# Score products of a graph layer per batch, with high and low parts side by side in one stationary block

## What is computed

```python
z_l = h @ W_lang.T;  z_g = h @ W_grav.T;  v = h @ W_V.T
zn  = z_l / max(norm(z_l), EPS)
A_l = max(zn @ zn.T, 0) * not_eye                        # 64 x 64 for each batch
d2  = max(sq + sq.T - 2 * z_g @ z_g.T, 0)                # sq = row sums of z_g * z_g
A_g = exp(-d2 / (2 * sigma**2)) * not_eye
K   = w * rows(A_l * causal) + (1 - w) * rows(A_g * causal)   # rows divided by their sums
out = (K @ v) @ W_O.T
x   = layernorm(x + out)
```

## Time and profile before

| | |
|---|---|
| median of 3 runs | 684.94 us (684.61 to 684.97) |
| profiled execution, its own time | 685.29 us |
| its span | 683.5 us, mean granted clock 0.996 |

### The profile page before, as it was taken

The page is one execution under the profiler, slowest core; times in us unless marked ns, Lnnn a source line. Parts: engine busy times, 40 slices in busy tenths (PEclk is TensorE's granted clock), DMA queues, the critical chain, the costliest instruction groups (busy, mean ns, idle before and its releaser), DMA issues.

```text
span 683.5 us, 11745 instructions
## 1 busy us (share of the span) xinstructions
PE 669.0 (98%) x3579; PEld 571.0 (84%) x3579; DVE 532.2 (78%) x1523; ACT 345.6 (51%) x614; POOL 210.4 (31%) x454
## 2 busy tenths in 40 slices
PE   7999999999999999999999999999999999999994
PEld 6888888888888888888888888888888888888883
DVE  5935697878879787887968787796978779697786
ACT  4734445464454546455454645545474554545433
POOL 0222315051341515134151513416051331503022
PEclk9999999999999999999999999999999999999998
DMA  7201102011110201111020111102011110001002
GB/s 280 107 7 57 61 32 94 1 62 63 56 68 31 92 0 61 61 61 61 31 92 0 64 59 61 61 31 92 0 66 57 61 61 31 32 0 63 1 31 94
DMA packets 20406, 38.33 MB, mean 56 GB/s; under 512 B 1824, under 2 KB 1824, under 8 KB 20384
## 3 DMA queue, kind: packets, MB, share of 16 engines
q1 hardware_dynamic: 20384, 38.05, 15.3%
HBM read 21.27 MB, written 16.78 MB: 56 GB/s over the span
## 4 chain that ended last, share of the span: by engine, by line
PE 92%; DVE 3%; ACT 2%; DMA 1%; issue 1%; POOL 1%; SPq 0%; POOLq 0%; DVEq 0%
PE ring L357 56%; PE bank_p L377 12%; PE ring L475 4%; PE bank_x L318 3%; PE bank_p L318 3%; PE bank_k L421 3%; PE bank_r L421 3%; PE bank_pt L390 2%; PE bank_r L397 1%; DMA w_raw<-in_L_gnn_W_lang_dram 1%; PE bank_pt L336 1%; PE bank_r L336 1%; PE bank_k L336 1%; PE bank_pt L408 1%; PE bank_x L336 1%
## 5 line engine op out<-in xcount | busy, mean ns | idle before, releaser
L562 ACT ACTIVATE yT_hi<-ring 128x512 fp32r<-128x512 f32 x128 | 75.9, 593 | 113.5 <-PE ring L357 113.3
L357 PE MATMUL ring<-hT_hi,T_hi 128*128 128x512 f32 x320 | 130.5, 408 | 0.6 <-DVE hT_lo L772 0.5
L357 PE MATMUL ring<-hT_hi,T_lo 128*128 128x512 f32 x320 | 125.4, 392 | 0.0
L357 PE MATMUL ring<-hT_lo,T_hi 128*128 128x512 f32 x320 | 124.7, 390 | 0.0
L777 DVE TENSOR_TENSOR yT_lo<-ring,yT_hi 128x512 fp32r<-128x512 f32 x128 | 87.5, 684 | 35.3 <-ACT yT_hi L562 35.3
L357 PE MATMUL ring<-M_hi,hT_hi 128*128 128x512 f32 x256 | 101.5, 396 | 0.0
L357 PE MATMUL ring<-M_hi,hT_lo 128*128 128x512 f32 x256 | 100.2, 391 | 0.0
L357 PE MATMUL ring<-M_lo,hT_hi 128*128 128x512 f32 x256 | 99.9, 390 | 0.0
L1084 POOL TENSOR_SCALAR z_ve<-z_mv 128x2 f32<-128x2 f32 x32 | 7.0, 218 | 268.8 <-DVE z_mv L873 264.1
L1077 POOL TENSOR_TENSOR x_lo<-x_sb,x_hi 128x512 fp32r<-128x512 f32 x60 | 76.4, 1301 | 22.4 <-ACT x_hi L562 22.4
L614 ACT ACTIVATE o_sb<-o_sb,z_nb,z_rs 128x512 f32<-128x512 f32 x60 | 47.2, 810 | 62.3 <-POOL z_nb L1089 62.3
(11 more groups left out here) (159 smaller groups left out, 1390.6 us busy)
## 6 DMA issues: line engine op xcount, KB each, us to landing
x_sb<-in_x_dram SPq DMA_DIRECT2D x15, 1024.0 KB, 5.2
out_dram<-o_sb SPq DMA_DIRECT2D x60, 256.0 KB, 2.0
x_sb<-in_x_dram SPq DMA_DIRECT2D x2, 512.0 KB, 5.5
w_raw<-in_L_gnn_W_lang_dram SPq DMA_DIRECT2D x1, 1024.0 KB, 6.7
o_sb<-in_L_gnn_W_grav_dram SPq DMA_DIRECT2D x1, 1024.0 KB, 9.4
h_sb<-in_L_gnn_W_V_dram SPq DMA_DIRECT2D x1, 1024.0 KB, 11.6
w_raw<-in_L_gnn_W_O_dram SPq DMA_DIRECT2D x1, 1024.0 KB, 7.9
out_dram<-x_sb SPq DMA_DIRECT2D x4, 256.0 KB, 2.0
```

The source lines that it names most:

```text
L357: last = pe.matmul(bank[:, :], a, b, start=n == 0, stop=n == len(terms) - 1)
L562: return act.activation(dst, src, ACT.Copy, scale=scale)
```

## The change

`gram` before had one 128 x 128 stationary block for each of high and low `hT` and did 3 x 4 matmuls of 256 columns a pair (24 for a call). After, `hT` holds for each pair the four blocks [high of batch 0, low of batch 0, low of batch 1, high of batch 1], 64 columns each, so that a stationary block of 128 columns is the high and the low part of one batch; the moving operand is [y high, y low] x [L, G] x 64 columns of the same batch. That is 2 x 4 matmuls of 256 columns a pair, 16 for a call, and only the diagonal blocks are computed. The result has the four quarters high·high, high·low, low·high and low·low in different partitions and columns. ACT copies the high rows (`Q_sb`, two copies of 64 x 512), POOL adds high·high and high·low (`Q_sum`), and DVE adds low·high from PSUM and writes P (`merge`, two instructions of 64 x 256). ACT also copies the high parts of `hT` into a contiguous `hU`, which is the stationary block of the u projections. The result of a call takes two PSUM banks, so the banks of `transpose_h` move, and the second `gram` of a step waits for the `merge` of the first.

```diff
+        hT = [sb(f"hT{i}", [R, DC, NP, 4, N], fp32r) for i in range(2)]
+        hT_hi = [t[:, :, :, 0:4:3, :] for t in hT]
+        hT_lo = [t[:, :, :, 1:3, :] for t in hT]
+        hU = sb("hU", [R, DC, GT], fp32r)
+        yT = sb("yT", [R, DC, 2, 2, GT], fp32r)
...
+                elif p == 3:
+                    pe.wait_ge(hT_split, NP * g + 1)
...
                 elif q:
-                    pe.wait_ge(p_copied, 2 * g + q)
+                    pe.wait_ge(p_merged, 2 * g + q)
...
                 for pp in range(2):
-                    s = slice((2 * q + pp) * R, (2 * q + pp + 1) * R)
-                    terms = [(a[:, i, s], b[:, i, :, s]) for i in range(DC)
-                             for a, b in parts(hT_hi[par], hT_lo[par], yT_hi, yT_lo)]
-                    for n, (a, b) in enumerate(terms):
-                        last = pe.matmul(p_bank(g, q)[:, pp, :, :], a, b, start=n == 0, stop=n == len(terms) - 1)
+                    p = 2 * q + pp
+                    for b in range(2):
+                        t = slice((2 * p + b) * N, (2 * p + b + 1) * N)
+                        for i in range(DC):
+                            last = pe.matmul(q_banks(g, q)[:, pp, b, :, :, :], hT[par][:, i, p, 2 * b:2 * b + 2, :],
+                                             yT[:, i, :, :, t], start=i == 0, stop=i == DC - 1)
...
+            def copy_hU(g, par, p):
+                act.wait_ge(hT_hi_done, NP * g + p + 1)
+                copy(hU[:, :, p * R:(p + 1) * R].rearrange("p c (b t) -> p c b t", b=2),
+                     hT_hi[par][:, :, p, :, :]).then_inc(hU_ready, 1)
...
+            def copy_q(g, q):
...
+                    act.wait_ge(q_summed, 2 * g + q)
+                for b in range(2):
+                    rows = slice(b * N, (b + 1) * N)
+                    last = copy(Q_sb[rows, :, :, :, :], q_banks(g, q)[rows, :, b, :, :, :])
+                last.then_inc(q_copied, 1)
...
                 hi_proj(g, 5)
+                copy_hU(g, par, 0)
+                copy_hU(g, par, 1)
                 hi_proj(g, 6)
+                copy_hU(g, par, 2)
+                copy_hU(g, par, 3)
                 hi_proj(g, 7)
...
+            def merge(g, q):
+                dve.wait_ge(q_summed, 2 * g + q + 1)
...
+                for b in range(2):
+                    rows, other = slice(b * N, (b + 1) * N), slice((1 - b) * N, (2 - b) * N)
+                    last = dve.tensor_tensor(P_sb[q][rows, :, :, rows], q_banks(g, q)[other, :, b, 0, :, :],
+                                             Q_sum[rows, :, :, :], ALU.add)
+                last.then_inc(p_merged, 1)
...
+            def sum_q(g, q):
+                d = 2 * g + q
+                pool.wait_ge(q_copied, d + 1)
...
+                pool.tensor_tensor(Q_sum[:, :, :, :], Q_sb[:, :, 0, :, :], Q_sb[:, :, 1, :, :],
+                                   ALU.add).then_inc(q_summed, 1)
...
+                    sum_q(g - 1, 1)
                     columns(g - 1, 1)
...
+                sum_q(g, 0)
                 columns(g, 0)
```

More of the change, by code:

```diff
@@ L98, in bass_two_layer_graph_resnorm @@
         h_sb = [sb(f"h_sb{i}", [R, NP, D]) for i in range(2)]
[L100 to L104, removed]
+        hT = [sb(f"hT{i}", [R, DC, NP, 4, N], fp32r) for i in range(2)]
[3 more added lines that the diff above has]
+        yT = sb("yT", [R, DC, 2, 2, GT], fp32r)
         u_hi = sb("u_hi", [R, NP, D], fp32r)
         u_lo = sb("u_lo", [R, NP, D], fp32r)
+        Q_sb = sb("Q_sb", [R, 2, 2, 2, N])
+        Q_sum = sb("Q_sum", [R, 2, 2, N])
         P_sb = [sb(f"P_sb{q}", [R, 2, 2, R]) for q in range(2)]
@@ L241, in bass_two_layer_graph_resnorm, with is_last, q_banks, hT_bank @@
         block = ctx.enter_context(nc.Block())
-        def p_bank(g, q):
-            return last_p_ps if isinstance(g, int) and g == NG - 1 and q else p_ps
+        def is_last(g):
+            return isinstance(g, int) and g == NG - 1
+        def q_banks(g, q):
+            return last_q_ps if is_last(g) and q else q_ps
+        def hT_bank(g, p):
+            if isinstance(g, int) and g == 0:
+                return (bank_x, bank_k, bank_pt, bank_r)[p]
+            return (bank_pt, bank_k, bank_r, bank_pt)[p]
+        def row_bank(g):
+            return last_row_ps if is_last(g) else row_ps
         def out_rows(g):
@@ L313, in layer0 @@
                     pe.wait_ge(y_added, NP * g + p - 1)
-                elif p == 1 and not (isinstance(g, int) and g < 2):
-                    pe.wait_ge(p_copied, 2 * g - 2)
+                elif p == 0 and not (isinstance(g, int) and g < 2):
+                    pe.wait_ge(p_merged, 2 * g - 2)
                 bank = (bank_x, bank_p)[p % 2]
@@ L362, in gram @@
                 pe.wait_ge(proj_split, NPROJ * g + 2 * DC)
-                if isinstance(g, int) and g == NG - 1:
-                    if not q:
-                        pe.wait_ge(p_copied, 2 * g)
+                if is_last(g):
+                    if q:
+                        pe.wait_ge(z_added, NP * g)
+                    else:
+                        pe.wait_ge(p_merged, 2 * g)
                 elif q:
-                    pe.wait_ge(p_copied, 2 * g + q)
+                    pe.wait_ge(p_merged, 2 * g + q)
                 else:
@@ L556, in proj_dst @@
                 return (u_hi, u_lo)[which][:, j, :]
-            return (yT_hi, yT_lo)[which][:, j, kind, :]
+            return yT[:, j, which, kind, :]
         @block.scalar
@@ L589, in hi_proj @@
                 copy(proj_dst(k, 0), ring[ring_of(k)][:, :]).then_inc(proj_hi, 1)
-            def copy_p(g, q):
+            def copy_q(g, q):
                 act.wait_ge(gram_done, 2 * g + q + 1)
-                if not (isinstance(g, int) and g == 0):
-                    act.wait_ge(s2_done, 2 * g + q - 1)
-                copy(P_sb[q][:, :, :, :], p_bank(g, q)).then_inc(p_copied, 1)
+                if not (isinstance(g, int) and g == 0 and q == 0):
+                    act.wait_ge(q_summed, 2 * g + q)
[3 more added lines that the diff above has]
+                last.then_inc(q_copied, 1)
             def exp_g(g, q):
@@ L888, in step @@
                 if tail:
+                    merge(g - 1, 1)
                     diagonals(g - 1, 1)
@@ L924, in step @@
                 lo_proj(g, 10)
-                diagonals(g, 0)
                 lo_hT(g + 1, 1 - par, 0)
                 lo_hT(g + 1, 1 - par, 1)
+                merge(g, 0)
                 lo_proj(g, 11)
@@ L930, in step @@
                 lo_hT(g + 1, 1 - par, 3)
+                diagonals(g, 0)
+            dve.wait_ge(p_zeroed, 2)
             dve.wait_ge(ident_ready, 2)
@@ L1037, in _ @@
             count_z(g - 1, 0)
+            merge(g, 0)
             diagonals(g, 0)
             count_z_pair(g - 1, 2)
+            merge(g, 1)
             add_p(g, 0)
@@ L1130, in _ @@
             pool.memset(pow_neg_half[:, :], -0.5)
+            for q in range(2):
+                pool.memset(P_sb[q][:, :, :, :], 0.0).then_inc(p_zeroed, 1)
             pool.memset(floors[0][:, 2:4], EPS)
@@ L1144, in _ @@
             g = NG - 1
+            sum_q(g - 1, 1)
             columns(g - 1, 1)
             scale_z(g - 1, 0)
+            sum_q(g, 0)
+            sum_q(g, 1)
             columns(g, 0)
```

93 lines of the change are left out of this document (55 added, 38 removed).

## The result

The changed kernel takes 720.55 us (median of 4 runs, 719.66 to 721.10), the kernel before 684.82 beside it: 1.052 times as long, 95% interval 1.0504 to 1.0535. The forecast was 710 with a range of 688 to 734. The span of the profiled execution grew from 683.5 to 717.9, by 34.4 us.

The account below looks back on a forecast made before the run. PE bound the kernel before; after, a ring of DVE and POOL would, 24.90 + 16.44 = 41.34 us a period against 39.65. The terms 4.6 + 17.7 + 1 - 1 + 2.6 = 24.9 gave 710 us, range 688 to 734.

Parts of the forecast that it names:

- PE's gain: On PE, 16 matmuls a gram instead of 24 save 1.91 us a step, 30.6 us in all, leaving 37.7 a step.
- the rival that PE stays the bound: PE still bounds the changed kernel, so the 30.6 us come in nearly whole: 655 to 660 us; chance 0.11.
- step 6 of the prediction: DVE's `diagonals(g, 0)`, now behind the `x_lo`, runs at full speed: 1.10 us from its start to that of `columns`.
- the first part of DVE's step: DVE from projection 0's low part to the end of `y_mv`: 24.57 us, growing 0.33 by `hU` copies to 24.90.
- Steps 1 to 4: From `y_mv`'s end: scale and shift 2.00, four `x_lo` 5.10, `sum_q` 0.80, first merge 0.85 us; POOL ends last.
- step 14: Loop step without `x_lo`, its second part bound by ACT's copies: -1 us, from between -3.6 and 0.
- Steps 4 to 6: On DVE: first merge 0.85, remaining low parts of projection 11 and `hT` 1.80, `diagonals` up to `columns` 1.10 us.
- Step 7: POOL's `columns(g, 0)`, ahead of the second `sum_q`: 1.64 us.
- Steps 8 and 9: Second `sum_q` on POOL 0.80, then on DVE second merge 0.85 and `diagonals(g, 1)` 1.50 us.
- Group 15: Last group, nothing else covering the path: projection 8 starts at 24.1 instead of 21.6 us, forecast as +2.6.
- The rival of the clock: PE's waits bring its clock to 1.2 GHz each step, 2.4 us a step, 31 us in all: 741 us; chance 0.07.
- the second parts of steps 1 to 13: DVE from `y_mv`'s end to the next projection 0: 16.44 us against 15.08, 13 x 1.36 = 17.7 us in all.

Follow-up runs that it names:

- before16_diagonals_behind: Kernel before with 16 instead of 24 matmuls a gram and DVE's `diagonals(g, 0)` moved behind the four low parts of `hT`: 654.3 us (0.955).
- before_16_matmuls: Kernel before with the low `hT` by high `y` product left out of the scores, 16 matmuls a gram, nothing else changed: 690.99 us (1.008).
- hU_copies_early: Changed kernel with ACT's four `hU` copies behind the high parts of projections 0, 1 and 2 instead of 5 and 6: 708.72 us (1.0345).
- xlo_next_step: Changed kernel with POOL's four `x_lo` moved from the end of a step to behind `columns(g - 1, 1)` of the next: 770.26 us (1.124).
- x_split_midstep: Changed kernel with `x_hi` and `x_lo` moved from the end of a step into the middle of the next: 705.86 us (1.0305).

## Why the prediction was right, and where it was short

**What bounds the kernel.** Right in the main: PE before, and after the change a ring, that is a circle of engines of which each waits for another's last work and which PE's own work doesn't fill. Its period is 41.91 (41.34 forecast; before, the mean is 39.76, read as 39.65). But it runs over ACT as well as DVE and POOL, and ACT I had left out.

**PE's gain.** Right in size, shown by `before16_diagonals_behind`: 37.72 a period. That run has DVE's order of the change and none of the added work, so the rival that PE stays the bound was rightly judged by the sum of the added steps. Two things I had not seen. In the order of before the gain would not have come in even with nothing added (`before_16_matmuls`), so moving `diagonals` was worth more than step 6 of the prediction says. And I wrote that the rows show hardly a wait in the first part of DVE's step that could go; 0.5 us of it did go (`hU_copies_early`).

**Steps 1 to 4, up to the first merge.** Wrong in the reason, and right in the number by luck. I put `Q_sum` last and the low parts of `hT` 0.4 us ahead of it. The merge began at 8.06 instead of 7.9, behind those low parts, and `xlo_next_step` shows that it does so with no `x_lo` ahead of `Q_sum`. Two paths are almost equally long here, 0.24 us apart; the one over ACT (`x_hi`, copies of the scores, normalising, copy of `hT`) I had not walked. Hence step 14, too: without `x_lo` I expected -1 and got +0.7. `Q_sum` began 3.60 us behind `y_mv` there, but the merge stood at 7.03, behind the same low parts.

**Steps 4 to 6.** From the first merge on, `sq_floor` came at 11.84, that is 3.78 behind the merge; 0.85 + 1.80 + 1.10 = 3.75 were forecast.

**Step 7.** Mis-sized: from `sq_floor` to the second `Q_sum` 1.98 us in most steps, not 1.64 (2.15 in the step shown, with a wait of 0.41 for ACT's copies behind the slow gram). `columns(g, 0)` takes 1.75, as it did in the kernel before; the 1.64 that I read in the earlier trace rows are those of `columns(g, 1)`. The sum starts 0.23 behind it, where I had 0.05; I tried nothing that tells the cause of that gap.

**Steps 8 and 9**: 3.1 us from the second `Q_sum` to the low part of projection 0, as forecast (0.80 + 0.85 + 1.50). The two halves of a merge take 0.86 and the next instruction starts 0.03 later (324.53 + 0.86, 325.42), where others overlap by 0.08. The Trainium skill's VectorE: DVE Perf Modes, section "Two Vector instructions with no wait between them", has such instructions held in turn; the trace agrees, and pricing whole durations was right.

**`hU`.** The total was right by two errors: 0.79 of cost for 0.33, and 0.5 of waiting for PE that went away.

**Group 15**, +4.5 instead of +2.6 (by its own terms the forecast is 24.05 - 21.57 = 2.5). PE waited 4.24 us behind the second gram, then ran at the lower clock (PE's row, and the window behind it):

```profile
691.15 1.09 PE L422 MATMUL bank_pt<-ident,P_sb 128*128 128x128 f32 x4 [4.24 <-DVE P_sb L856]
```

```profile
691.15:696.05 4.90, 4.90 (x18) 4.15 (x19) 4.65 (x24) 0.51 (x1) 2.49 (x7) 0.68 0.13 48
```

These transposes and projection 8 took 4.9 us where they took 3.4 before (658.50 to 659.15 + 2.74): 1.5 of the 1.9 that were missing. Ahead of it, the last instruction of `diagonals`, for which PE waited, ran beside POOL's second `Q_sum` and took 0.81 us instead of 0.29 (DVE's row, then POOL's):

```profile
689.60 0.81 DVE L848 CUSTOM_DVE_ANT_0 diag_scr<-P_sb,ident 128x128 f32<-128x128 f32 x1
```

```profile
689.40 0.86 POOL L1186 TENSOR_TENSOR Q_sum<-Q_sb 128x256 f32<-128x256 f32 x1 [1.36 <-ACT Q_sb L596]
```

Both were only read: no experiment kept PE busy there or parted the two. The rival of the clock was thus right in this place and wrong in the steps.

**The number.** The 9.5 us by which the span grew beyond the forecast are 6.5 in the second parts of steps 1 to 13 (0.16 a step ahead of the first merge, 0.34 at step 7), 1.7 in step 14, 1.9 in group 15 and 0.6 in step 0, less 0.7 in the first parts and 0.4 ahead of step 0. The profiled execution was the shortest of the four; the median lies 0.9 above it.

## What to carry to other kernels

Before work is moved off the engine that bounds, walk every path of the ring that it gates, not only the one that the change touches, and give the saving once for free (leave the work out) to see whether it comes in: here that gave 691 us, and with one call moved in DVE's queue 654. If the time gets longer, look at the granted clock too: part of the loss can be the clock that a new wait brought down. Then count the new work by its place in each in-order queue: the same changed kernel ran at 770, 720 or 665 us, by where `x_lo`, `x_hi`, `hU` and the second sum stood.

## What was unexpected of the hardware

- The pairing of VectorE and GpSimd is one-sided here: a row of four `x_lo` lets one VectorE instruction with two SBUF operands through for each (0.75 to 1.37 us instead of 0.29, in `xlo_next_step`), while the `x_lo` take 1313 ns instead of 1293.
- The same two waits, 1.25 and 0.77 us around four transposes, bring TensorE's granted clock to 0.54 in one step and leave it at 1.00 in the next, in the same execution. In `hU_copies_early` and `x_split_midstep`, where the first of the two waits is 0.2 to 0.5 us, the second gram runs at 1.00 in every step.
